# The order of VectorE's work around two residuals in a fused attention and mixture-of-experts kernel

## The reference

```python
x = x + xattn0(ctx, layernorm(x))          # 8 heads of 128, keys from both inputs
x = x + ffn0(layernorm(x))                 # 1024 wide, GELU, low-rank updates made from tokens
x = x + xattn1(layernorm(x), ctx, ctx)     # one head of 256, softmax over ctx
x = x + experts(layernorm(x))              # 8 experts, sum_e w[e] * (silu(x Wg[e]) * (x Wu[e])) Wd[e]
```

## Time and profile before

| | |
|---|---|
| median of 3 runs | 1988.76 us |
| lowest, highest | 1985.94, 1989.46 us |
| profiled execution, its own time | 1991.09 us |
| its span | 1989.3 us |
| granted TensorE clock over the span | 0.995 of full speed |
| busy: TensorE, weight loads, VectorE, ScalarE, GpSimd | 97, 91, 69, 56, 20% |

### The profile page before, as it was taken

The page is one execution under the profiler, slowest core; times in us unless marked ns, Lnnn a source line. Parts: engine busy times, 40 slices in busy tenths (PEclk is TensorE's granted clock), DMA queues, the critical chain, the costliest instruction groups (busy, mean ns, idle before and its releaser), DMA issues.

```text
span 1989.3 us, 41475 instructions
## 1 busy us (share of the span) xinstructions
PE 1927.2 (97%) x14078; PEld 1803.2 (91%) x14078; DVE 1367.9 (69%) x3408; ACT 1115.5 (56%) x2334; POOL 407.1 (20%) x650
## 2 busy tenths in 40 slices
PE   7999999999999999999987899999999999999998
PEld 6788888888888888888886899999999999999998
DVE  7877776776777776776746566766666666766665
ACT  5655565555655565555655655554555555544553
POOL 2222222222222222222213511111111101111100
PEclk9999999999999999999999999999999999999999
DMA  4000000000000000000012200000000000000000
GB/s 162 12 22 21 11 11 21 21 21 5 16 21 21 11 11 21 21 21 6 10 34 89 67 15 15 12 17 17 11 16 16 17 12 17 12 17 12 17 7 12
DMA packets 47211, 44.51 MB, mean 22 GB/s; under 512 B 6848, under 2 KB 45376, under 8 KB 47168
## 3 DMA queue, kind: packets, MB, share of 16 engines
q1 hardware_dynamic: 47168, 43.96, 6.9%
HBM read 34.77 MB, written 8.39 MB: 22 GB/s over the span
## 4 chain that ended last, share of the span: by engine, by line
PE 83%; DVE 7%; ACT 5%; issue 3%; POOL 1%; SPq 1%; DMA 0%; DVEq 0%; ACTq 0%; POOLq 0%
PE ring L618 9%; PE ring L620 9%; PE ring L619 9%; PE ring L1820 7%; PE ring L1818 7%; PE ring L1819 7%; PE ring L671 4%; PE sim L1818 3%; PE sim L1819 3%; PE sim L1820 3%; PE sim L618 3%; PE sim L620 2%; PE sim L619 2%; PE ps_x L1818 2%; PE ps_x L1820 2%
## 5 line engine op out<-in xcount | busy, mean ns | idle before, releaser
L411 ACT ACTIVATE a_pr<-sim,a_nmax 128x512 f32<-128x512 f32 x256 | 174.5, 689 | 208.4 <-DVE a_nmax L537 208.3
L1818 PE MATMUL ring<-b_xch,b_weh 128*128 128x256 f32 x1024 | 289.5, 283 | 1.7 <-DVE b_act_e L1464 1.7
L1819 PE MATMUL ring<-b_xcl,b_weh 128*128 128x256 f32 x1024 | 285.7, 279 | 0.0
L1820 PE MATMUL ring<-b_xch,b_wel 128*128 128x256 f32 x1024 | 285.6, 279 | 0.0
L326 POOL TENSOR_SCALAR a_pr<-a_pr,a_rinv 128x512 f32<-128x512 f32 x256 | 183.1, 729 | 498.3 <-DVE a_rinv L547 495.4
L1818 PEld LDWEIGHTS ring<-b_xch,b_weh 128*128 128x128 f32 x1024 | 192.3, 188 | 1.9 <-DVE b_act_e L1464 1.9
L1819 PEld LDWEIGHTS ring<-b_xcl,b_weh 128*128 128x128 f32 x1024 | 193.0, 188 | 0.0
L1820 PEld LDWEIGHTS ring<-b_xch,b_wel 128*128 128x128 f32 x1024 | 192.1, 188 | 0.0
L1464 DVE TENSOR_TENSOR b_act_e<-b_act_e,ring 128x512 f32<-128x512 f32 x128 | 87.9, 687 | 116.7 <-PE ring L1820 102.4
L528 DVE TENSOR_TENSOR a_ptl<-ring,a_pth 128x512 fp32r<-128x512 f32 x256 | 163.9, 682 | 3.1 <-ACT a_pth L401 2.0
L515 DVE SCALAR_TENSOR_TENSOR a_ktl<-ring,a_bkv_s,a_kth 128x512 fp32r<-128x512 f32 x128 | 95.3, 744 | 102.1 <-ACT a_kth L391 102.1
(11 more groups left out here) (378 smaller groups left out, 6246.0 us busy)
## 6 DMA issues: line engine op xcount, KB each, us to landing
a_c_in<-in_ctx_in SPq DMA_DIRECT2D x16, 256.0 KB, 2.6
a_x_in<-in_x SPq DMA_DIRECT2D x16, 256.0 KB, 2.9
a_x_res<-in_x SPq DMA_DIRECT2D x16, 256.0 KB, 2.6
x_between<-a_x_out SPq DMA_DIRECT2D x16, 256.0 KB, 2.2
b_x_s<-x_between SPq DMA_DIRECT2D x16, 256.0 KB, 2.6
b_up<-b_ev SPq DMA_DIRECT2D x256, 1.0 KB
out_x<-b_acc SPq DMA_DIRECT2D x16, 256.0 KB, 2.2
b_ct_raw<-in_ctxT SPq DMA_DIRECT2D x15, 256.0 KB, 2.6
```

The lines of the kernel that those rows point to most:

```text
L411: nc.scalar.activation(pr[:, h % 2, t, :], sim[t][:], ACT.Exp, bias=nmax[:, h % 2, t:t + 1], accum_out=rsum[:, h % 2, t:t + 1]).then_inc(e ...
L1818: nc.tensor.matmul(out, lh, rh, start=(n == 0), stop=False)
L1819: nc.tensor.matmul(out, lh, rl, start=False, stop=False)
L1820: last = nc.tensor.matmul(out, ll, rh, start=False, stop=(n == len(parts) - 1 and not more))
```

## The change

On VectorE alone, in the turns of the second half, two groups of instructions are moved. The second residual and the statistics of norm B go ahead of hidden(3). The third residual and the statistics of norm C go ahead of hidden_low(6) and with it ahead of weigh(5). Nothing is added or taken away, and the other engines' lists stay as they are.

```diff
@@ -1746,10 +1746,10 @@
                         g_low(t, k)
                 weigh(i, 1)
 
-                hidden(i, 3)
                 if chain:
                     second_residual(t)
                     norm_stats(t, "B", x2_s)
+                hidden(i, 3)
                 hidden_low(i, 3)
                 if chain:
                     norm_apply(t, "B", x2_s)
@@ -1785,11 +1785,11 @@
                     copy_low(t, "T", hl[:, PT, 0:S], hh[:, PT, 0:S])
                 if more:
                     copy_low(t + 1, "A", xtl[:], xth[:])
+                if chain:
+                    third_residual(t)
+                    norm_stats(t, "C", x2_s)
                 hidden_low(i, 6)
                 weigh(i, 5)
-                if chain:
-                    third_residual(t)
-                    norm_stats(t, "C", x2_s)
 
                 hidden(i, 7)
                 if chain:
```

More of the change, by code:

```diff
@@ L1787, in turn @@
                     copy_low(t + 1, "A", xtl[:], xth[:])
-                hidden_low(i, 6)
-                weigh(i, 5)
                 if chain:
@@ L1792, in turn @@
                     norm_stats(t, "C", x2_s)
+                hidden_low(i, 6)
+                weigh(i, 5)
                 hidden(i, 7)
```

## The result

The changed kernel takes 1999.18 us (median of 6 runs, 1997.07 to 1999.88) against 1988.76 us (6 runs too, 1985.94 to 1989.46): ratio 1.0053, 95% interval 1.0040 to 1.0066, or 8.0 to 13.1 us more. The forecast was 1998.5 us, in a range of 1995.0 to 2003.0. The profiled execution of the changed kernel took 1999.74 us, 8.65 us more than the profiled one of before.

A forecast was written before the change was run, and what follows sets the result against it. TensorE was taken to bound the kernel, with recurring pauses before the norm B and C transposes. Losses of 0.9 and 8.85 us, 9.75 together, added to the 1988.76 median gave 1998.5 us, range 1995.0 to 2003.0.

The forecast's parts named there:

- What bounds the kernel: TensorE, busy 97% of the span; only its idle moments before the norm B and norm C transposes matter.
- Edit 1: Norm B: residual and statistics ahead of hidden(3); normalisation 0.06 us later per turn, waiting behind hidden_low(3); 0.9 us in all.
- GpSimd's first operation: At norm B, beside hidden(3) instead of hidden_low(3), it falls from 0.43 to 0.19 us, changing nothing in the sum.
- Edit 2: Norm C: residual and statistics ahead of hidden_low(6) and weigh(5); hidden(7) and normalisation 0.59 us late per turn, 8.85 us.
- Sum: Both places over 15 turns: 0.9 + 8.85 = 9.75 us, added to the median 1988.76, giving 1998.5 us.
- Rival 1: At norm C, weigh(5) also holds off GpSimd's 0.70 us operation: another 2.9 us, 2001.4 us; chance 0.08.
- Rival 2: Norm B: hidden_low(3) off the path, gaining 6 to 9.6 us against Edit 2's 8.85; 1988.0 to 1991.7; chance 0.06.
- Rivals 3 and 4: Spare VectorE time at norm C makes it faster, 1982.8 us, chance 0.03; or TensorE's stalls cancel, no change, 1988.8, chance 0.05.

The follow-up runs named there:

- edit 1 with the normalisation ahead of hidden_low(3): Against the kernel before: second residual and norm B's statistics ahead of hidden(3), norm B's normalisation ahead of hidden_low(3); 1980.32 us, ratio 0.9955.
- edit 1 alone: Against the kernel before: only the second residual and norm B's statistics go ahead of hidden(3); 1990.99 us, ratio 1.0006.

## Why the prediction was right

- *What bounds the kernel.* TensorE's two recurring pauses in the turns. Right: 8.0 of the span's 8.7 us are in their rows and in the one new wait that was named.
- *Edit 1, 0.06 us a turn.* Right. Measured 0.08, inside the bounds of 0.03 and 0.09, but not by the way that gave the bounds. The residual starts 0.43 sooner, for which the prediction's sum gives 0.03; three small steps add 0.05: hidden(3) comes 0.20 after the aggregation where 0.17 was taken, hidden_low(3) 0.04 after ScalarE where 0.03 was, the normalisation 0.61 after hidden_low(3) where 0.60 was. The late instruction is hidden_low(3), as named. This is shown by edit 1 with the normalisation ahead of hidden_low(3), which differs from edit 1 alone in nothing else.
- *GpSimd's first operation.* 0.43 was foretold to fall to 0.19 us, without effect on the sum. Both hold. The Trainium skill ("SBUF — State Buffer", section "Who interferes with whom") says that a VectorE instruction with two SBUF inputs contends with a GpSimd instruction that reads SBUF. All nine traces agree, in every turn: 0.43 beside hidden_low, 0.19 beside hidden, beside weigh(5) or beside an idle VectorE.
- *Edit 2, 0.59 us a turn.* The mechanism was right (0.81 us of spare time, 1.40 of work, two pauses that share the loss), the size a little too large: 0.52. The three VectorE instructions follow each other more closely here: hidden_low to weigh 0.57 for 0.60, weigh to hidden 0.79 for 0.80, hidden to normalisation 0.59 for 0.61. down(6) is 0.28 late, 0.31 was said (0.21 of it shows as idle time before its weight load). The lower end of the prediction (0.50) had named closer packing.
- *Sum.* 9.75 us forecast; 0.59 x 15 = 8.9 us by the traces and 10.4 by the medians. The difference between these two is how far each profiled execution lies from its median (2.3 us above before, 0.6 after). Where that comes from is not shown; the traces do show 2.0 us of variation ahead of the turns. That 1998.5 and 1999.18 lie so close is partly luck: the sum was 0.9 us too large by the traces, and the median it was added to, 1988.76, came out 1.0 us higher in the 21 later runs (1989.76), which leaves 9.4 us of loss.
- *Rival 1*, GpSimd held off by weigh(5): out. GpSimd's second operation starts at 1328.85, inside weigh(5) (1328.63 to 1329.50), and takes its usual 0.70 us. What the rival says in general, that GpSimd can become the bound at C, does happen in the kernel with hidden_low(6) alone behind, where hidden(7) is not late; there it is hidden_low(6) that holds GpSimd's first operation, not weigh(5) its second.
- *Rival 2* is out by edit 1 alone: hidden_low(3) was on the path. *Rivals 3 and 4* are out by the result: the third residual still waits for `o_fill` (1.31 us of idle time before it), and nothing else took up the loss.

## What to carry to other kernels

Moving an instruction up an in-order queue moves all others down: look for what the moved group waits for (here `o_fill`; other work had been done during that wait at no cost), and for what stands between it and the result that it is to bring forward (here hidden_low(3), one hand-over to ScalarE and back). Here the early start of the chain was worth nothing until its last step was released early too: with that step moved, the kernel gained 9.4 us instead of losing 1.2. Spare time acts as a threshold: 0.79 us of work fitted into 0.81 at no cost, 0.57 us cost 0.10 for another reason (what it did to GpSimd), and the two together cost 0.52 per turn.

## What the runs showed of the hardware that was not expected

An instruction that is on nobody's path can cost time by what runs beside it. For hidden_low(3) this was expected: finished 0.86 us too early, its removal from GpSimd's company gave 0.23 us in each turn, 3.5 us over 15 (4.4 us by the medians). Not expected was the same at C, where hidden_low(6) alone, put into time that VectorE had to spare, cost 0.10 us in each turn, about the 0.11 by which the normalisation came later behind hidden(7).

The rows show the interference between VectorE and GpSimd: 0.43 against 0.19 us for an operation of 2 elements on 128 partitions, which ends 0.05 us after the VectorE instruction does (1326.01 + 0.66 = 1326.67 and 1326.72). Two other GpSimd operations show it too. A copy of 32 elements (L1057) takes 0.50 us beside hidden_low(6) and 0.21 where edit 2 takes hidden_low(6) away; over 14 turns that is 4.1 of the 5.6 us that GpSimd's total lost. And L1050 went from 1.29 to 1.68 us, as said above. All these VectorE instructions are hidden_low, with both inputs in SBUF. An instruction of VectorE with the same output format and one input in PSUM (L1493) runs beside a GpSimd operation of 512 elements (L1044) that takes 1.31 us, about what L1050 takes undisturbed, so the output format is not what does it.
